# An xDeepFM forward pass on one core: layer 1 of the last five pairs as three fp32r terms

## The chip, the cores and the metric

One core of one Trainium2 chip runs the program. The metric is the device time of one execution in microseconds; the median of three runs is compared. Engines are named as in the profile: PE is the matrix engine, DVE VectorE, ACT ScalarE, POOL GpSimd, SP the engine that issues most DMAs.

## The reference, cut to what matters

512 samples, 26 sparse features with embeddings of 32 values, 13 dense values.

```python
emb = tables[feat_idx, sparse]                      # (512, 26, 32)
linear_out = lin_sparse_w[feat_idx, sparse].sum(-1) + dense @ lin_dense_w
x0 = xk = emb
for w, bb in ((conv1_w, conv1_b), (conv2_w, conv2_b)):   # CIN, 128 outputs each
    hp = einsum('bhd,bmd->bhmd', xk, x0).reshape(-1, h * 26, 32)
    xn = sigmoid(einsum('oi,bid->bod', w, hp) + bb)
    xk = xn[:, :64]; res.append(xn[:, 64:])
cin_out = concatenate(res, 1).sum(-1) @ cin_w + cin_b
h1 = tanh([emb, dense] @ W1 + b1)                   # 845 -> 1024
h2 = tanh(h1 @ W2 + b2)                             # -> 512
h3 = tanh(h2 @ W3 + b3)                             # -> 256
out = linear_out + cin_out + h3 @ deep_w + deep_b + bias
```

## The kernel before, in words

The batch is cut into 16 pairs (NPAIR) of 32 samples. A pair is two chunks c of 16 samples, so 2 x 512 columns of (sample, embedding value).

Gathering: POOL fetches the rows of a pair into emb by seven indirect DMAs (L396); its queue holds the gathers of all 16 pairs first. SP writes them to HBM as laid (L309, L311), and reads them back as raw (L331) and, one feature broadcast over 64 partitions, as copied (L344). For the pairs 0 and 1 SP lays them out directly (L319). ACT (x_high, L640) and DVE (x_low, L766) split raw into a high fp32r part and the rest, both in the tile x.

Layer 1 of the CIN works on squares: a product of two features comes from the square of their sum. PE makes the sums of pairs of features from x with 0/1 weights (sums_of, L455), ACT squares them (squares, L649) into sq, three tiles u of 117 rows for each c, and PE multiplies sq with the weights in fp32 (layer1, L473), two column halves q of 64 outputs each. ACT takes two sigmoids into xk (L660) and one into res1 (L662).

Layer 2 has 13 tiles t per pair. Each needs a product of xk with two features of x, spread over the partitions: in the tiles 2, 3, 6, 7, 8, 11, 12 (COPIED) the features come by DMA into an SBUF buffer copied and DVE multiplies SBUF by SBUF; in the tiles 0, 1, 4, 5, 9, 10 (SPREAD) PE spreads them into PSUM (spread_tile, L485) and DVE multiplies PSUM by SBUF (both L836). PE then multiplies with the weights in fp32 (main, L495), four matmuls a tile in the count of the profile. res2 is taken by ACT (sigmoid2, L670); DVE sums res1 and res2 over the embedding (fold1 L774, fold2 L780), and transposes emb for the deep network (turn, L793, L794).

The order on PE of a pair i is written by hand in three groups: sums(i+1,2), spread tiles 4 and 5, main 0 to 3, layer1(i+1,0); then sums(i+2,0), spread 9 and 10, main 4 to 8, layer1(i+1,1); then sums(i+2,1), spread 0 and 1 of pair i+1, main 9 to 12. Sums and spread tiles share a ring of three PSUM buffers, so spread 9 waits for the product of tile 4 and spread 10 for that of tile 5 (slot_free). DVE starts the products of a pair when the sigmoids of layer1(i,1) are in xk. DVE does x_low(i+2) after tile 5, fold1 after tile 5, turn and fold2(i-1) after tile 9. ACT's order in pair i is sigmoid2(i-1), squares(i+1,2), x_high(i+2), a weight piece, sigmoid(i+1,0), squares(i+2,0), sigmoid(i+1,1), squares(i+2,1).

The deep network runs as three fp32r terms: hi x hi, lo x hi, hi x lo (deep, L516). The weights of its first layer come as 14 pieces of 512 columns, one a pair: SP loads one, ACT writes hi (piece_high, L677), DVE writes lo after tile 11 (piece_low, L787). Its input xt is split in pair 15: hi by ACT (L726), lo by POOL (xt_low, L405), started at the products 0, 4 and 9 of that pair. The first deep tile is worked in between the groups of pair 15; the rest follows, and POOL splits the weights of the later layers beside it (split_piece, L411, L413).

Before the first pair PE multiplies 12 times with unused results (WARM, L545), and twice more after layer1(0,1) (L562).

## Time and profile before

| what | us |
|---|---|
| median of three runs | 420.84 (420.27 to 423.86) |
| the profiled execution, its own time | 420.59 |
| span of its instructions | 418.8 |
| PE busy in the span | 402.7 |
| DVE busy | 311.9 |

The span runs from the first to the last instruction of the profiled execution; 1.8 us lie around it. The clock granted to PE was 0.992 of full over the whole. Steady work begins near 61 us; from there a pair takes 19.42 us, and the last product of pair 15 is multiplied at 350.28 us. The deep network is what is left.

### The profile page before, as it was taken

The numbers are of one execution on the slowest core, as the hardware profiler recorded it, in microseconds if no ns is written. First come the engines' busy times: TensorE is split into PE (matmuls) and PEld (weight loads), VectorE is DVE, ScalarE is ACT, GpSimd is POOL, SyncE is SP. The second block draws the span as 40 slices with busy tenths as digits, with TensorE's granted clock in tenths as the row PEclk, the third lists the DMA queues.
The fourth block names the chain that finished last, engine by engine and source line by source line (L and its number), as shares of the span: only waits on it lengthen the run. The fifth ranks groups of instructions, "written<-read, shape, count | busy, mean of one in ns | idle before, by whom it ended". The sixth has DMA issues, their size and how long they took to land.

```text
span 418.8 us, 5255 instructions
## 1 busy us (share of the span) xinstructions
PE 402.7 (96%) x1854; PEld 167.9 (40%) x1854; DVE 311.9 (74%) x347; ACT 161.9 (39%) x269; POOL 174.6 (42%) x146
## 2 busy tenths in 40 slices
PE   3967999999999999999999999999999999999998
PEld 1412233333333333333333333333333335887885
DVE  4104869998989989898989898998989898432223
ACT  3136445435253544544543525354454511112012
POOL 6745473664844754855656600000000255880000
PEclk9979999999999999999999999999999999999999
DMA  5368689999999999999989998899978670430000
GB/s 203 60 142 177 159 185 227 212 237 235 216 230 224 220 236 237 224 235 212 234 227 219 228 226 233 211 221 214 227 189 200 167 186 2 122 79 2 1 0 2
DMA packets 43582, 73.93 MB, mean 177 GB/s; under 512 B 22206, under 2 KB 24638, under 8 KB 43555
## 3 DMA queue, kind: packets, MB, share of 16 engines
q1 hardware_dynamic: 39970, 71.82, 71.5%
q0 software_dynamic: 3584, 1.76, 3.2%
q8 instruction: 15, 0.25, 0.3%
q14 instruction: 13, 0.10, 0.1%
HBM read 71.63 MB, written 1.71 MB: 175 GB/s over the span
## 4 chain that ended last, share of the span: by engine, by line
PE 88%; issue 4%; ACT 2%; another core or an unknown queue 2%; DMA 1%; SPq 1%; DVE 1%; DVEq 0%; ACTq 0%
PE conv L495 43%; PE conv L473 19%; PE conv L516 8%; PE ring L516 7%; PE ring L485 5%; PE ring L455 4%; ACT xk L660 1%; SPq L319 1%; PE ring L531 1%; ACT x L632 1%; DMA idx_sb<-in_idx 0%; ACT res L662 0%; DMA copied<-emb 0%; DVE prod L836 0%
## 5 line engine op out<-in xcount | busy, mean ns | idle before, releaser
L396 POOL DMA_INDIRECT emb<-in_table,rows x112 | 141.9, 1267 | 96.9 <-DMA emb<-in_table,rows 65.2
L836 DVE TENSOR_TENSOR prod<-ring,xk 128x1024 f32<-128x1024 f32 x96 | 114.2, 1216 | 32.3 <-ACT xk L660 27.4
L836 DVE TENSOR_TENSOR copied<-copied,xk 128x1024 f32<-128x1024 f32 x112 | 135.1, 1243 | 0.0
L495 PE MATMUL conv<-copied,w_sb 128*64 128x512 f32 x448 | 105.2, 593 | 0.0
L660 ACT ACTIVATE xk<-conv,const_sb 64x512 f32<-64x512 f32 x64 | 43.7, 683 | 143.1 <-PE conv L473 117.0
L495 PE MATMUL conv<-prod,w_sb 128*64 128x512 f32 x384 | 93.1, 605 | 2.7 <-DVE prod L836 2.7
L473 PE MATMUL conv<-sq,w_sb 117*64 117x512 f32 x384 | 90.7, 608 | 3.4 <-ACT sq L689 3.4
L495 PEld LDWEIGHTS conv<-copied,w_sb 128*64 128x64 f32 x448 | 31.7, 137 | 63.5 <-issue 55.8
L473 PEld LDWEIGHTS conv<-sq,w_sb 117*64 117x64 f32 x384 | 27.7, 139 | 58.8 <-issue 57.7
L405 POOL TENSOR_TENSOR xt_lo<-xt,xt_hi 128x512 fp32r<-128x512 f32 (+1 forms) x7 | 10.9, 1582 | 96.2 <-ACT xt_hi L726 91.6
L649 ACT ACTIVATE sq<-ring 117x512 f32<-117x512 f32 x90 | 48.6, 595 | 3.9 <-issue 3.2
L495 PEld LDWEIGHTS conv<-prod,w_sb 128*64 128x64 f32 x384 | 23.3, 136 | 47.3 <-issue 42.8
L485 PE MATMUL ring<-x,sel_sb 58*128 58x512 f32 x192 | 32.1, 407 | 0.7 <-ACT sq L649 0.7
L875 DVE CAST h_hi<-hf 128x512 fp32r<-128x512 f32 x8 | 8.2, 1024 | 21.7 <-ACT hf L739 21.7
L455 PEld LDWEIGHTS ring<-x,sel_sb 58*117 58x117 f32 x96 | 8.4, 174 | 36.6 <-issue 35.7
L670 ACT ACTIVATE res<-conv,const_sb 128x512 f32<-128x512 f32 x16 | 11.1, 691 | 31.1 <-PE conv L495 27.9
L455 PE MATMUL ring<-x,sel_sb 58*117 58x512 f32 x96 | 22.9, 481 | 0.0
L662 ACT ACTIVATE res<-conv,const_sb 64x512 f32<-64x512 f32 x32 | 21.9, 684 | 0.8
L485 PEld LDWEIGHTS ring<-x,sel_sb 58*128 58x128 f32 x192 | 17.9, 188 | 10.6 <-issue 4.9
L761 DVE TENSOR_TENSOR x<-copied,x 26x512 fp32r<-26x512 f32 x4 | 2.8, 688 | 23.5 <-issue 15.1
L875 DVE CAST xt_hi<-hf 128x512 fp32r<-128x512 f32 x4 | 1.7, 427 | 17.9 <-ACT hf L739 17.9
L739 ACT ACTIVATE hf<-ring,const_sb 128x512 f32<-128x512 f32 x6 | 4.1, 689 | 26.0 <-PE ring L516 26.0
(99 smaller groups left out, 324.8 us busy)
## 6 DMA issues: line engine op xcount, KB each, us to landing
copied<-laid SPq DMA_DIRECT2D x224, 256.0 KB
wpiece<-in_mlp SPq DMA_DIRECT2D x22, 256.0 KB
raw<-laid SPq DMA_DIRECT2D x56, 52.0 KB
emb<-in_table,rows POOLq DMA_INDIRECT x112, 4.8
laid<-emb SPq DMA_DIRECT2D x16, 96.0 KB
sel_f<-in_sel SPq DMA_DIRECT2D x1, 832.0 KB, 5.6
const_sb<-in_const SPq DMA_DIRECT2D x1, 626.5 KB, 4.1
w_sb<-in_w SPq DMA_DIRECT2D x1, 416.0 KB
```

Source lines behind the costliest of these rows:

```text
L396: pool.indirect_dma_start(out=emb[0:n, i, j, :], out_offset=None, in_=table, in_offset=bass.IndirectOffsetOnAxis(ap=rows[0:n, i, j:j + 1], ...
L405: nc.gpsimd.tensor_tensor(xt_lo[0:n, k, :], xt[0:n, k, :], xt_hi[0:n, k, :].bitcast(F32), ALU.subtract).then_inc(xt_lo_done, 1)
L455: mm = nc.tensor.matmul(sums_bank(i, u)[0:UK, c, :], sel1_sb[at:at + XK, u, :], x[i % RX][at:at + XK, :], start=True, stop=True)
L473: mm = nc.tensor.matmul(l1_bank(i, c)[o, :], w1_sb[:, u, o], sq[i % 2][0:UK, u, c, :], start=(u == 0), stop=(u == UT - 1))
L485: mm = nc.tensor.matmul(spread_bank(r)[:, c, :], sel2_sb[at:at + XK, t, :], x[i % RX][at:at + XK, :], start=True, stop=True)
L495: mm = nc.tensor.matmul(conv[i % 2][c * HALF:(c + 1) * HALF, :], w2_sb[:, t, :], prod_of(r)[:, c, :], start=(t == 0), stop=(t == T2 - 1))
L516: mm = nc.tensor.matmul(MLP_BANKS[n % 2], w[0:r, k, mt * P:(mt + 1) * P], h[0:r, k, :], start=(k == 0 and j == 0), stop=(k == kt - 1 and j ...
L649: nc.scalar.activation(sq[i % 2][0:UK, u, c, :], sums_bank(i, u)[0:UK, c, :], ACT.Square)\
L660: nc.scalar.activation(xk[i % 2][q * HALF:(q + 1) * HALF, c, :], bank[0:HALF, :], ACT.Sigmoid, bias=small_sb[0:HALF, C_CB1:C_CB1 + 1]).the ...
L662: nc.scalar.activation(res1[i % 2][c * HALF:(c + 1) * HALF, :], bank[HALF:P, :], ACT.Sigmoid, bias=small_sb[HALF:P, C_CB1:C_CB1 + 1]).then ...
L670: nc.scalar.activation(res2[i % 2][:, :], conv[i % 2][:, :], ACT.Sigmoid, bias=small_sb[:, C_CB2:C_CB2 + 1]).then_inc(l2_read, 1)
L836: nc.vector.tensor_tensor(prod_of(r)[:, :, :].rearrange("p c n -> p (c n)"), left[:, :, :].rearrange("p c n -> p (c n)"), xk[i % 2][:, :, ...
```

## The change

Layer 1 of the pairs 11 to 15 (SPLIT_FROM) is no longer an fp32 product of 2 x 3 column halves but nine fp32r products over all 128 columns: w_hi x sq_hi and w_lo x sq_hi for each u, then w_hi x sq_lo. For this ACT writes sq_hi after each pair of squares (square_highs, two copies), and sq_lo is written over sq: five of the six tiles of a pair by POOL (LOWS), started when the products 0 (one), 4 (two) and 9 (two) of a pair are reached, and the sixth, (1, 1), by DVE after tile 3 (LOW_AT). The weight split w1_lo is one more instruction at the start.

The space for sq_hi is taken from the low parts of the deep weights. Two of the seven weight tiles (KEEP) are split as before, in four pieces in the pairs 1 to 4. The other five are loaded whole into the place of their high parts in the pairs 4 to 13, and split late, in two sets of five pieces: ACT copies a piece (late_copy), POOL or DVE makes the low part, ACT rounds the high part in place (late_high). The first set lies in pair 14 (two on POOL, three on DVE after tile 12) with its high parts in pair 15; the second lies behind the last product (all on DVE). The last of the seven xt_lo goes from POOL to DVE, after tile 8.

x_low is moved from behind tile 5 to behind tile 3 in the pairs from 1 on. WARM is 9 and the second filler runs once. SP issues the first two copies behind the direct layout of pair 1 instead of ahead of it.

```diff
@@ -50,8 +50,11 @@
 SPREADS_IN = (((0, 4), (0, 5)), ((0, 9), (0, 10)), ((1, 0), (1, 1)))
 SUMS_IN = {0: ((1, 2),), 1: ((2, 0),), 2: ((2, 1),)}
 L1_IN = {0: 0, 1: 1}
-X_LOW_AT, TURN_AT, FOLD1_AT, PIECE_AT = (10, 5), 9, (5, 5), 11
-WARM = 12
+X_LOW_AT, TURN_AT, FOLD1_AT, PIECE_AT = (10, 3), 9, (5, 5), 11
+KEEP = 2
+LOW_AT, LATE_AT, XT_AT = 3, 12, 8
+SPLIT_FROM = 11
+WARM = 9

 C_B1, C_B2, C_B3, C_DEEP, C_CB1, C_CB2, C_CIN1, C_CIN2, C_ONE, C_AUX, C_LOW, C_END = 0, 8, 12, 14, 16, 17, 18, 19, 20, 22, 23, 24
 SMALL_AT = 0
...
@@ -98,17 +102,25 @@
-        m1_hi = sb("m1_hi", [P, K1, D1], F32R)
-        m1_lo = sb("m1_lo", [P, K1, D1], F32R)
+        at_m1 = space(K1 * D1 * 4)
+        m1_hi = sb("m1_hi", [P, K1, D1], F32R, at_m1)
+        m1_f = sb("m1_f", [P, K1, D1], F32, at_m1)
+        m1_kept = sb("m1_kept", [P, KEEP, D1], F32R)
-        at_a = space(2 * K1 * B * 4)
-        sq = [sb(f"sq{k}", [P, UT, 2, CH], F32, at_a + k * UT * 2 * CH * 4) for k in range(2)]
-        xt_hi = sb("xt_hi", [P, K1, B], F32R, at_a)
-        xt_lo = sb("xt_lo", [P, K1, B], F32R, at_a + K1 * B * 4)
+        SQ = UT * 2 * CH * 4
+        LATE = (K1 - KEEP) * D1 * 4
+        at_a = space(4 * SQ)
+        assert LATE + 2 * K1 * B * 4 <= 4 * SQ and LATE <= 2 * SQ
+        sq_hi = [sb(f"sq_hi{k}", [P, UT, 2, CH], F32R, at_a + 2 * k * SQ) for k in range(2)]
+        sq = [sb(f"sq{k}", [P, UT, 2, CH], F32, at_a + (2 * k + 1) * SQ) for k in range(2)]
+        sq_lo = [sb(f"sq_lo{k}", [P, UT, 2, CH], F32R, at_a + (2 * k + 1) * SQ) for k in range(2)]
+        m1_late = sb("m1_late", [P, K1 - KEEP, D1], F32R, at_a)
+        xt_hi = sb("xt_hi", [P, K1, B], F32R, at_a + LATE)
+        xt_lo = sb("xt_lo", [P, K1, B], F32R, at_a + LATE + K1 * B * 4)
...
@@ -183,7 +200,10 @@
-        KW = 2 * K1
+        KW = 2 * KEEP
+        NL = K1 - KEEP
+        LATE_POOL = 2
+        LOWS = ((0, 0), (0, 1), (1, 0), (2, 0), (2, 1))
@@ -223,6 +243,17 @@

             return RAW * (i // RX + (1 if i % RX >= DIRECT else 0))

+        def late(m):
+
+            k, at = KEEP + m % NL, m // NL * WP
+            n = P if k < K1 - 1 else K1_LAST
+            return (m1_f[0:n, k, at:at + WP], mlp1[k * P:k * P + n, at:at + WP],
+                    m1_hi[0:n, k, at:at + WP], m1_late[0:n, k - KEEP, at:at + WP])
+
+        def m1_low(k):
+
+            return m1_kept[:, k, :] if k < KEEP else m1_late[:, k - KEEP, :]
+
@@ -352,11 +395,9 @@
             sp.dma_start(aux[DENSE_AT:DENSE_AT + ND, :], dense_t).then_inc(aux_in, 16)
             direct(0)
             lay_out(0)
-            for n in range(2):
-                copy(n)
             direct(1)
             lay_out(1)
-            for n in range(2, RC):
+            for n in range(RC):
                 copy(n)
             lay_out(2)
             fetch(2)
...

+            def sq_low(i, u, c):
+
+                pool.wait_ge(sq_hi_done, highs_up_to(i, u, c))
+                nc.gpsimd.tensor_tensor(sq_lo[i % 2][0:UK, u, c, :], sq[i % 2][0:UK, u, c, :],
+                                        sq_hi[i % 2][0:UK, u, c, :].bitcast(F32), ALU.subtract)\
+                  .then_inc(sq_lo_done, 1)
+
+            def late_low(m):
+
+                src, _, _, lo = late(m)
+                pool.wait_ge(late_copied, m + 1)
+                nc.gpsimd.tensor_tensor(lo, src, lo.bitcast(F32), ALU.subtract).then_inc(late_lo, 1)
+
...
@@ -418,15 +474,31 @@
+            for i in range(SPLIT_FROM - 2, NPAIR):
+                if SPLIT_FROM <= i + 1:
+                    pool.wait_ge(prod_done, T2 * i)
+                    if i + 1 < NPAIR:
+                        sq_low(i + 1, 1, 0)
+                    else:
+                        xt_low(0)
+                        xt_low(1)
+                    pool.wait_ge(prod_done, T2 * i + 4)
+                    if i + 1 < NPAIR:
+                        sq_low(i + 1, 2, 0)
+                        sq_low(i + 1, 2, 1)
+                    else:
+                        xt_low(2)
+                        xt_low(3)
+                pool.wait_ge(prod_done, T2 * i + 9)
+                if i + 2 < NPAIR:
+                    sq_low(i + 2, 0, 0)
+                    sq_low(i + 2, 0, 1)
+                elif i == NPAIR - 2:
+                    for m in range(LATE_POOL):
+                        late_low(m)
+                else:
+                    xt_low(4)
+                    xt_low(5)
@@ -466,12 +538,29 @@
                     pe.wait_ge(l1_read, 2 * i + 1)
                 if (i, c) == (0, 1):
                     pe.wait_ge(aux_read, 1)
+                bank = l1_bank(i, c)
+                if i < SPLIT_FROM:
+                    for u in range(UT):
+                        pe.wait_ge(sq_done, squares_up_to(i, u, c))
+                        for q in range(2):
+                            o = slice(q * HALF, (q + 1) * HALF)
+                            mm = nc.tensor.matmul(bank[o, :], w1a_sb[:, u, o], sq[i % 2][0:UK, u, c, :],
+                                                  start=(u == 0), stop=(u == UT - 1))
+                    mm.then_inc(l1_done, 1)
+                    return
                 for u in range(UT):
-                    pe.wait_ge(sq_done, squares_up_to(i, u, c))
-                    for q in range(2):
-                        o = slice(q * HALF, (q + 1) * HALF)
-                        mm = nc.tensor.matmul(l1_bank(i, c)[o, :], w1_sb[:, u, o], sq[i % 2][0:UK, u, c, :],
-                                              start=(u == 0), stop=(u == UT - 1))
+                    pe.wait_ge(sq_hi_done, highs_up_to(i, u, c))
+                    nc.tensor.matmul(bank[:, :], w1_hi[:, u, :], sq_hi[i % 2][0:UK, u, c, :],
+                                     start=(u == 0), stop=False)
+                    nc.tensor.matmul(bank[:, :], w1_lo[:, u, :], sq_hi[i % 2][0:UK, u, c, :],
+                                     start=False, stop=False)
+                for u in range(UT):
+                    if (u, c) in LOWS:
+                        pe.wait_ge(sq_lo_done, lows_up_to(i, u, c))
+                    else:
+                        pe.wait_ge(sq_lo_dve, i - SPLIT_FROM + 1)
+                    mm = nc.tensor.matmul(bank[:, :], w1_hi[:, u, :], sq_lo[i % 2][0:UK, u, c, :],
+                                          start=False, stop=(u == UT - 1))
                 mm.then_inc(l1_done, 1)

             def spread_tile(r):
...
@@ -506,14 +595,18 @@
+                if layer == 0:
+                    pe.wait_ge(late_hi, NL * (1 + mt * P // WP))
-                    if n == 0:
+                    if n == 0 and k < K1 - 1:
+                    elif n == 0:
...
@@ -558,7 +651,7 @@
-            for k in range(2):
+            for k in range(1):
@@ -649,6 +742,14 @@
+            def square_highs(i, u):
+
+                if i >= SPLIT_FROM:
+                    for c in range(2):
+                        act.wait_ge(sq_done, squares_up_to(i, u, c))
+                        nc.scalar.activation(sq_hi[i % 2][0:UK, u, c, :], sq[i % 2][0:UK, u, c, :], ACT.Copy)\
+                          .then_inc(sq_hi_done, 1)
+
@@ -669,6 +770,21 @@
+
+            def late_copy(m):
+
+                src, _, _, lo = late(m)
+                act.wait_ge(late_in[m // NL], 16 * NL)
+                nc.scalar.activation(lo, src, ACT.Copy).then_inc(late_copied, 1)
+
+            def late_high(m):
+
+                src, _, hi, _ = late(m)
+                if m < LATE_POOL:
+                    act.wait_ge(late_lo, m + 1)
+                else:
+                    act.wait_ge(late_lo_dve, m - LATE_POOL + 1)
+                nc.scalar.activation(hi, src, ACT.Copy).then_inc(late_hi, 1)
@@ -705,18 +821,25 @@
                 sigmoid2(i - 1)
                 if i + 1 < NPAIR:
                     squares(i + 1, 2)
+                    square_highs(i + 1, 2)
                 if i + 2 < NPAIR:
                     x_high(i + 2)
                 if i <= KW:
                     piece_high(i - 1)
+                if i == NPAIR - 2:
+                    act.wait_ge(l1_done, 2 * (NPAIR - 1))
+                    for m in range(NL):
+                        late_copy(m)
                 if i + 1 < NPAIR:
                     sigmoid(i + 1, 0)
                 if i + 2 < NPAIR:
                     squares(i + 2, 0)
+                    square_highs(i + 2, 0)
                 if i + 1 < NPAIR:
                     sigmoid(i + 1, 1)
                 if i + 2 < NPAIR:
                     squares(i + 2, 1)
+                    square_highs(i + 2, 1)
                 if i == NPAIR - 2:
                     act.wait_ge(l1_done, 2 * NPAIR)
                     act.wait_ge(turned, 2 * NPAIR)
@@ -725,9 +848,15 @@
                         n = P if k < K1 - 1 else K1_LAST
                         nc.scalar.activation(xt_hi[0:n, k, :], xt[0:n, k, :], ACT.Copy).then_inc(xt_hi_done, 1)

+            for m in range(NL):
+                late_high(m)
+            for m in range(NL, 2 * NL):
+                late_copy(m)
             sigmoid2(NPAIR - 1)
             act.wait_ge(lin_done, 1)
             nc.scalar.activation(lin16[:, :], ring[1][0:NPAIR, 1, 0:PB], ACT.Copy).then_inc(lin_copied, 1)
+            for m in range(NL, 2 * NL):
+                late_high(m)

             n = 0
             for layer, bias in enumerate((C_B1, C_B2, C_B3)):
@@ -840,6 +984,16 @@
+                    if t == LOW_AT and SPLIT_FROM <= i + 1 < NPAIR:
+                        sq_low(i + 1, 1, 1)
+                    if t == LATE_AT and i == NPAIR - 2:
+                        for m in range(LATE_POOL, NL):
+                            late_low(m)
+                    if t == XT_AT and i == NPAIR - 1:
+                        dve.wait_ge(xt_hi_done, K1)
+                        nc.vector.tensor_tensor(xt_lo[0:K1_LAST, K1 - 1, :], xt[0:K1_LAST, K1 - 1, :],
+                                                xt_hi[0:K1_LAST, K1 - 1, :].bitcast(F32), ALU.subtract)\
+                          .then_inc(xt_lo_dve, 1)
@@ -854,6 +1008,8 @@
+            for m in range(NL, 2 * NL):
+                late_low(m)
```

In pair i, PE waits in a split layer1 for highs_up_to and, in the last three matmuls, for lows_up_to or sq_lo_dve.

## Rows read from the trace of the kernel before

**Rows 1.** The page, part 1: busy time, share of the span, instructions.
```profile
PE 402.7 (96%) x1854; PEld 167.9 (40%) x1854; DVE 311.9 (74%) x347; ACT 161.9 (39%) x269; POOL 174.6 (42%) x146
```

**Rows 2.** The page, part 4: the chain that ended last, by line.
```profile
PE conv L495 43%; PE conv L473 19%; PE conv L516 8%; PE ring L516 7%; PE ring L485 5%; PE ring L455 4%; ACT xk L660 1%; SPq L319 1%; PE ring L531 1%; ACT x L632 1%; DMA idx_sb<-in_idx 0%; ACT res L662 0%; DMA copied<-emb 0%; DVE prod L836 0%
```

**Rows 3.** The timeline, PE, pair 10: start us, us, engine line op.
```profile
232.69 0.49 PE L455 MATMUL ring<-x,sel_sb 58*117 58x512 f32 x2
...
241.52 2.75 PE L473 MATMUL conv<-sq,w_sb 117*64 117x512 f32 x12
244.20 0.49 PE L455 MATMUL ring<-x,sel_sb 58*117 58x512 f32 x2
...
245.08 1.94 PE L495 MATMUL conv<-prod,w_sb 128*64 128x512 f32 x8
...
252.10 0.49 PE L455 MATMUL ring<-x,sel_sb 58*117 58x512 f32 x2
```

**Rows 4.** The timeline, DVE, pair 10.
```profile
234.23 2.36 DVE L836 TENSOR_TENSOR prod<-ring,xk 128x1024 f32<-128x1024 f32 x2 [1.80 <-ACT xk L660]
236.50 2.35 DVE L836 TENSOR_TENSOR copied<-copied,xk 128x1024 f32<-128x1024 f32 x2
...
241.03 0.74 DVE L766 SCALAR_TENSOR_TENSOR x<-raw,const_sb,x 122x512 fp32r<-122x512 f32 x1
241.70 0.68 DVE L774 TENSOR_REDUCE fold<-res 128x16 f32<-128x512 f32 x1
...
246.83 0.37 DVE L793 STREAM_TRANSPOSE xt<-emb 128x192 f32<-128x192 f32 x1
...
247.21 0.63 DVE L780 TENSOR_REDUCE fold<-res 128x16 f32<-128x512 f32 x1
...
250.04 0.68 DVE L787 TENSOR_TENSOR m_lo<-wpiece,m_hi 128x512 fp32r<-128x512 f32 x1
```

**Rows 5.** The chain in order of time, last part of pair 15: start us, us.
```profile
350.28 2.29 PE conv L516 x9
```

**Rows 6.** The timeline, ACT, pair 10.
```profile
234.93 1.08 ACT L649 ACTIVATE sq<-ring 117x512 f32<-117x512 f32 x2
...
238.81 0.64 ACT L640 ACTIVATE x<-raw 122x512 fp32r<-122x512 f32 x1
```

**Rows 7.** The timeline, ACT, pair 15.
```profile
331.80 3.75 ACT L726 ACTIVATE xt_hi<-xt 128x512 fp32r<-128x512 f32 x7
```

**Rows 8.** The timeline, POOL, pair 15, two looks at single instructions.
```profile
332.58 1.29 POOL L405 TENSOR_TENSOR xt_lo<-xt,xt_hi 128x512 fp32r<-128x512 f32 x1 [91.58 <-ACT xt_hi L726]
...
333.83 2.28 POOL L405 TENSOR_TENSOR xt_lo<-xt,xt_hi 128x512 fp32r<-128x512 f32 x1
```

**Rows 9.** The timeline, DVE, pair 15, looks at single instructions.
```profile
333.37 1.58 DVE L836 TENSOR_TENSOR copied<-copied,xk 128x1024 f32<-128x1024 f32 x1
...
334.88 2.31 DVE L836 TENSOR_TENSOR copied<-copied,xk 128x1024 f32<-128x1024 f32 x1
...
337.11 1.21 DVE L836 TENSOR_TENSOR prod<-ring,xk 128x1024 f32<-128x1024 f32 x1
```

**Rows 10.** Windows, pairs 14 and 15: us, busy time by engine, PEclk, DMA, GB/s.
```profile
310.36:329.56 19.20, 19.20 (x94) 6.42 (x92) 17.31 (x20) 7.36 (x12) 0.00 (x0) 1.00 0.75 188
329.56:352.50 22.94, 22.94 (x104) 8.95 (x102) 20.89 (x19) 7.17 (x12) 10.89 (x7) 1.00 0.53 130
```

**Rows 11.** The timeline, the head, PE and DVE.
```profile
8.50 12.15 PE L545 MATMUL conv<-sel_f 128*128 128x512 f32 x24
...
21.53 0.96 PE L455 MATMUL ring<-x,sel_sb 58*117 58x512 f32 x6
...
35.05 1.98 PE L562 MATMUL ring<-w_sb 128*128 128x512 f32 x4
...
17.69 1.40 DVE L761 TENSOR_TENSOR x<-copied,x 26x512 fp32r<-26x512 f32 x2 [8.36 <-ACT x L632]
```

**Rows 12.** One tile's instructions, h_hi: ns min/median/max.
```profile
L875 DVE CAST h_hi<-hf x8: 426/1358/1465, 353.8 to 387.3; 128x512 fp32r<-128x512 f32 x8
```

62 lines of the change are left out of this document (40 added, 22 removed).

## The prediction

> **What bounds the kernel now.** I read the busy table first: PE is busy 402.7 of 418.8 us, DVE 311.9, ACT 161.9 [rows 1]. The chain that ended last stands on PE for its large parts, 43% main and 19% layer 1 [rows 2], and DVE's products, its last line, hold 0%. The reader is to see in pair 10 how near the second engine is. I take as zero the start of sums(12,1), 232.69; the same point of the next pair is 252.10 [rows 3], so a pair takes 19.42 us, all PE work. In it layer 1 of one c starts at 8.83 and the next work on PE at 11.51: 2.68 us, twice a pair; main 4 starts at 12.39 [rows 3], 0.88 later, the price of sums and two spread tiles. A tile of main is what is left, (19.42 - 2 x 2.68 - 3 x 0.88) / 13 = 0.88. DVE has 13 products at 1.135 (two in 2.27), x_low 0.67, fold1 0.60, turn 0.38, fold2 0.56 and piece_low 0.60 [rows 4]: 14.76 + 2.81 = 17.57 us. It waits 1.80 us for xk, and starts tile 0 at 1.54 [rows 4]. So DVE has 1.8 us to spare in 19.4. What is new in the pairs 10 to 14 is that POOL, silent there once its gathers are done, computes beside DVE; only pair 15 shows what that costs.
>
> **The split layer 1.** Nine fp32r matmuls after main took 2.29 us, 350.28 on, those of the deep network with nearly the same shape [rows 5]. Against 2.68 that saves 0.39, ten times (two for each of the pairs 11 to 15, worked in PE's pairs 10 to 14): 3.9 us, if PE never waits. PE's own work in a pair becomes 19.42 - 0.78 = 18.64 us.
>
> **ACT.** Six more copies a pair; seven took 3.75 us, 0.54 each [rows 7], so 3.2 us on an engine with over 9 us free. The squares (i+1,1) are issued at 2.24 and take 1.08 [rows 6]; the first copy behind them is done at 3.9. x_high starts at 6.12 and takes 0.64 [rows 6]; two copies now stand ahead of it: done at 6.12 + 1.08 + 0.64 = 7.84. The copies of (i+2,0) and (i+2,1) fall in the gaps before the next sigmoids.
>
> **POOL beside DVE.** In pair 15 a low part on POOL takes 1.29 us, beside a product from PSUM (1.21, its usual) [rows 8, 9]. The next one began at 333.83 and took 2.28; DVE's two SBUF products around it took 1.58 and 2.31 instead of 1.21 [rows 8, 9]. Laid end to end this is one at a time: POOL to 333.88, product, POOL, product. So an operation of DVE with two SBUF inputs and one of POOL go in turn, each whole. x_low and the DVE sq_low also have two SBUF inputs; that they queue too no row shows. Bounds for what the two lows after tile 3 cost DVE there: 0, and 2.66 as worked below. I take 2.66, since the nearest rows are SBUF by SBUF. The Trainium skill, SBUF — State Buffer, section "Who interferes with whom", says that a DVE instruction with two SBUF inputs and a GpSimd one that reads SBUF exclude each other for the whole instruction, the first to start having the port. By this rule the sum is my forecast; with a port that only the wide products feel it is the fast rival below.
>
> **A pair from 10 to 13, step by step** (from the pair's zero). POOL's low part of the square tile u = 1, c = 0 of the next pair, written (i+1,1,0), is free to start at product 0 but waits for the copy at 3.9: it works 3.93 to 5.22. In pair 10 DVE is on time, tile 2 has the port at 3.81, POOL goes 4.94 to 6.23, tile 3 ends at 7.36. In the later pairs DVE is late, tile 2 waits until 5.22 and tile 3 ends at 7.49. Now DVE wants x_low, which needs x_high: 7.84. POOL wants (i+1,2,0), released by the same tile 3, at 7.57, and has the port until 8.86. x_low to 9.53, POOL's second low to 10.82, sq_low to 11.42. Without POOL that is 7.49 + 1.27 = 8.76: cost 2.66. Tile 4 ends at 12.56, tile 5 at 13.69. PE's spread 10 waits for tile 5, where PE would be there at 11.7 (8.83 + 2.29 + about 0.6); one spread tile later, at 14.05, main 4 starts; five tiles 4.39, 0.1 for tile 8, layer 1 2.29: the next zero at 20.83, xk at 22.37. DVE after tile 5 has 0.60 + 3.40 + 1.13 + 0.94 + 3.40 = 9.48 and ends at 23.17, 0.80 late. That fits its own sum: 17.57 (sq_low in place of piece_low) + 0.61 before tile 2 + 2.66 = 20.84. The two lows after tile 8 fall beside tiles 9 and 10, from PSUM: nothing. So pair 10 takes 20.7, pairs 11 to 13 20.84: 83.2 against 77.7, **+5.5 us**. The saved PE time is gone and DVE sets the pace.
>
> **Pair 14** has no x_low, so the DVE sq_low has the port first, 7.49 to 8.09, and POOL's lows lie beside tiles 4 and 5. PE: 19.20 [rows 10] - 0.78, **-0.8 us**.
>
> **Pair 15.** In pair 14 DVE goes on from 8.09 with 9.48 + 2.27 + 0.38 for the second turn and ends at 20.2, 1.8 us after the next zero at 18.42. Three late lows of 0.60 follow before tile 0; xk was ready at 1.54. If POOL's first xt_low, free at 2.95, comes behind the third, tile 1 ends at 5.9 instead of 3.9; if before it, at 7.2. Spread 5 wants it near 4.4 (0.9 and four tiles). Bounds 0 and +2.8; I take **+1.3** on the 22.94 [rows 10], as the race is even and 1.5 is its good end, less what small waits of today it swallows. late_high on ACT ends near 9.4 (xt_hi at 2.24 + 3.75, then sigmoid2 and five copies), PE wants it at 8.6 + 1.3: covered. The second late set: DVE's five (3 us) after the products delay ACT's five copies and so the first tanh by some 3 us, but deep tile 1 (21 matmuls, near 5 us) is worked meanwhile: 0; uncovered it would be 3.
>
> **The head.** 12 fillers run 8.50 to 20.65, and the sums start at 21.53; they need x_low, done at 17.69 + 1.40 = 19.09 [rows 11]. Three fillers less are 3.0 us at their mean of 1.01, of which 2.4 counts. The other filler: 2 took 1.98 [rows 11], behind layer1(0,1); one less saves 0 to 0.99, I take 0.9. **-3.3 us**, bounds 0 (if something else holds the first squares back) and -4.0 (all four in full). The split of w1 is one 0.5 us operation on an idle DVE. The first two copies are needed some 20 us after their old issue: 0; the direct layout of pair 1 and its gathers get free earlier. x_low behind tile 3 in the pairs 1 to 9 waits 0.7 for x_high, out of DVE's 1.8: 0, and 0.7 a pair if that were used up.
>
> **Sum**: 420.6 - 3.3 + 5.5 - 0.8 + 1.3 = **423.3 us** for the profiled execution. Its 420.59 is within 0.3 of the median, 420.84, so I give the same. My bound of what can be told from no change is 1%: 416.6 and 425.0.
>
> **The rivals.** *x_low wins the race* after tile 3: only 0.27 us decide. For it: ACT and POOL latencies of 0.1 are my guess. Against: pair 10 has 0.4 in POOL's favour. Then x_low ends at 8.16, POOL 9.45, sq_low 10.05, tile 5 12.32: 1.37 less in four pairs, 5.5: **417.8**. *The port hardly matters for x_low and sq_low*: PE stays the bound, four pairs at 18.64 are -3.1, pair 14 -0.8, pair 15 +0.5, head -3.3: **413.9**. For it: no row shows these operations blocked. Against: the products were, exactly in turn. *Slower*: the two lows after tile 8 also block turn and fold2, one-input operations. For it: the DVE cast of h_hi, one input, took 1358 ns beside POOL, 426 alone [rows 12]. They would stand between the two lows and wait 0.2 + 1.3 = 1.5 us in each of the pairs 10 to 13, where DVE has nothing left: +6.0, **429.3**. It decides as soon as turn starts while POOL works, at 18.8 against 19.0. Against: alone, the cast takes 0.43 us for 512 columns and the reduction 0.63 [rows 4, 12], so they are not the same kind of work. The same section of the Trainium skill says that only the two-port modes of DVE, and two SBUF inputs, exclude GpSimd, and a reduction never does; by it this rival costs nothing. *The change doesn't act*: PE's fp32r layer 1 as slow as fp32 would take 3.9 from the fast cases and nothing from mine, where DVE is the bound.
>
> **How the numbers follow.** Forecast 0.42, its own range 421 to 426.5; x_low first 0.16; free port 0.24; slower 0.10; near 420 from mixtures 0.08. The range goes from 413 to 428, which leaves out the slow rival and less than a tenth below. Faster by over 1%: the free port and some of x_low first, 0.28. Slower: 0.10 and 0.13 from the upper part of the forecast, 0.23. Within: 0.49.
>
> **What would show it.** Zeros of the pairs 10 to 14 some 20.8 us apart, DVE with no idle in them; x_low and sq_low of DVE at about 1.3 to 1.9 us in place of 0.7; PE waiting before L485 for DVE in each; layer 1 at 2.3 us; pairs 2 to 9 unchanged at 19.42; steady work 3.3 us earlier. Wrong: pairs near 18.6, or fold2 stretched to 1.9.

## The result and the profile after

Beside each other on one chip, the changed kernel took 431.77 us (431.14 to 432.56) and the kernel before 421.55 us: ratio 1.023, 95% interval 1.019 to 1.027. It is slower, by some 10 us. I had said 423.3, within 1% of before. A second comparison on another chip gave the same ratio (after_2, 1.023, 1.018 to 1.029). Ratios, here and below, leave out executions over 1.5% above the fastest of the same kernel, among them single ones of 685 to 1045 us, of the kernel before too.

The page of the changed kernel, part 1 (against [rows 1]), and the start of part 4, the chain by engine:

```profile
PE 404.2 (94%) x1816; PEld 174.3 (41%) x1816; DVE 327.1 (76%) x352; ACT 183.9 (43%) x309; POOL 203.2 (47%) x172
PE 79%; DVE 6%; ACT 4%; issue 3%; another core or an unknown queue 3%; POOL 2%; DMA 1%; DVEq 0%; ACTq 0%; POOLq 0%
```

PE's busy time is no lower, though its layer 1 got shorter and four fillers are gone: it stood at half clock for 20.5 us in three stretches, against 6.8 us before. DVE has 15 us more.

The profiled execution took 432.04 us against 420.59, 11.45 more. I laid it out by four marks in both timelines: the start of tile 0 of pair 2 on DVE, the zeros of pair 10 and of pair 14 on PE (the start of the sums from which the prediction counts), and the linear term's first matmul behind pair 15.

| stretch | before | after | difference | predicted |
|---|---|---|---|---|
| start to tile 0 of pair 2 | 78.86 | 83.04 | +4.2 | -3.3 |
| from there to the zero of pair 10 | 153.83 | 153.87 | 0.0 | 0 |
| pairs 10 to 13 | 77.67 | 84.81 | +7.1 | +5.5 |
| pairs 14 and 15, to the linear term | 42.14 | 42.23 | +0.1 | +0.5 |
| deep layers, to the end | 66.28 | 66.28 | 0.0 | 0 |

So the split's pairs came out as forecast in kind and 1.6 us dearer, and the head came out 7.5 us over its forecast: it lost 4.2 us instead of gaining 3.3.

First the pairs. PE, timeline of pair 12 of the changed kernel, the lines that answer to [rows 3]:

```profile
280.47 0.49 PE L527 MATMUL ring<-x,sel_sb 58*117 58x512 f32 x2
...
289.41 0.50 PE L553 MATMUL conv<-sq_hi,w_hi 117*128 117x512 f32 x1
...
290.90 0.86 PE L562 MATMUL conv<-sq_lo,w_hi 117*128 117x512 f32 x3
291.69 0.49 PE L527 MATMUL ring<-x,sel_sb 58*117 58x512 f32 x2
292.50 0.49 PE L574 MATMUL ring<-x,sel_sb 58*128 58x512 f32 x2 [0.32 <-DVE prod L980]
293.63 0.50 PE L574 MATMUL ring<-x,sel_sb 58*128 58x512 f32 x2 [0.64 <-DVE prod L980]
...
300.91 0.49 PE L527 MATMUL ring<-x,sel_sb 58*117 58x512 f32 x2
```

Layer 1 of one c runs from 289.41 to 291.69, 2.28 us: the 2.29 that I had taken from the deep layers [rows 5]. Behind it stand two waits for DVE's products. The pair takes 20.44 us.

DVE (answering to [rows 4]) and POOL in the same pair, two timelines:

```profile
284.27 3.44 DVE L980 TENSOR_TENSOR copied<-copied,xk 128x1024 f32<-128x1024 f32 x2
288.30 1.31 DVE L895 SCALAR_TENSOR_TENSOR x<-raw,const_sb,x 122x512 fp32r<-122x512 f32 x1 [0.59 <-ACT x L733]
289.54 1.77 DVE L921 TENSOR_TENSOR sq_lo<-sq,sq_hi 117x512 fp32r<-117x512 f32 x1
...
297.50 1.21 DVE L980 TENSOR_TENSOR prod<-ring,xk 128x1024 f32<-128x1024 f32 x1
298.63 0.36 DVE L934 STREAM_TRANSPOSE xt<-emb 128x192 f32<-128x192 f32 x1
...
299.02 0.63 DVE L909 TENSOR_REDUCE fold<-res 128x16 f32<-128x512 f32 x1
```

```profile
284.58 2.05 POOL L447 TENSOR_TENSOR sq_lo<-sq,sq_hi 117x512 fp32r<-117x512 f32 x1 [6.43 <-ACT sq_hi L750]
287.79 2.98 POOL L447 TENSOR_TENSOR sq_lo<-sq,sq_hi 117x512 fp32r<-117x512 f32 x2 [1.16 <-ACT sq_hi L750]
297.65 2.53 POOL L447 TENSOR_TENSOR sq_lo<-sq,sq_hi 117x512 fp32r<-117x512 f32 x2 [6.89 <-DVE copied L980]
```

The reader is to see three things. Two SBUF products take 3.44 us instead of 2.35, where POOL's first low part begins. x_low takes 1.31 and DVE's sq_low 1.77, where they would be 0.74 and 0.68, while POOL works 287.79 to 290.77. And beside POOL's last two, 297.65 to 300.18, the transpose (0.36) and the reduction (0.63) are as short as in [rows 4].

Now pair 10, POOL's timeline, and what DVE did beside it:

```profile
228.44 1.42 POOL L439 DMA_INDIRECT emb<-in_table,rows  x1 [5.14 <-DMA emb<-in_table,rows]
...
239.14 0.90 POOL L439 DMA_INDIRECT emb<-in_table,rows  x1 [0.30 <-issue]
240.14 3.77 POOL L447 TENSOR_TENSOR sq_lo<-sq,sq_hi 117x512 fp32r<-117x512 f32 x3
```

```profile
240.72 5.41 DVE L980 TENSOR_TENSOR copied<-copied,xk 128x1024 f32<-128x1024 f32 x2
240.72 4.28 DVE L980 TENSOR_TENSOR copied<-copied,xk 128x1024 f32<-128x1024 f32 x1
246.06 0.74 DVE L895 SCALAR_TENSOR_TENSOR x<-raw,const_sb,x 122x512 fp32r<-122x512 f32 x1
```

The last set of gathers ends at 240.04 and three low parts that were free to start run in one go. DVE's first SBUF product waits for all three (the second line is that product alone): 5.41 - 2.35 = 3.06 us lost. With tile 3 that late, x_high is there, and x_low starts ahead of POOL's next low part (246.06 against 246.21) and takes 0.74: the one pair with low parts in this trace in which x_low comes first. From the start of tile 0 of pair 10 to that of pair 11 it is 21.69, not 20.7. (From here on "pair n" gives this distance from tile 0 to tile 0 on DVE; in it PE works layer 1 of pair n + 1. Pair 11 takes 21.85: a stretch of 3.4 us at half clock from 272.3 on is in it, behind waits of PE for DVE of 0.68 and 0.64 us; pair 13 has nearly the same waits and no such stretch. Pairs 12 and 13 take 20.98 and 20.81.)

The head: the timelines of PE and ACT in the changed kernel.

```profile
19.54 0.96 PE L527 MATMUL ring<-x,sel_sb 58*117 58x512 f32 x6
24.00 1.98 PE L547 MATMUL conv<-sq,const_sb 117*64 117x512 f32 x4 [3.51 <-issue]
26.32 3.68 PE L547 MATMUL conv<-sq,const_sb 117*64 117x512 f32 x8 [0.34 <-ACT sq L805]
29.93 0.74 PE L574 MATMUL ring<-x,sel_sb 58*128 58x512 f32 x4
...
40.22 0.78 PE L527 MATMUL ring<-x,sel_sb 58*117 58x512 f32 x2 [5.77 <-DVE x L890]
```

```profile
23.26 0.60 ACT L805 ACTIVATE sq<-ring 117x512 f32<-117x512 f32 x1 [4.95 <-remote]
25.67 0.60 ACT L805 ACTIVATE sq<-ring 117x512 f32<-117x512 f32 x1 [1.81 <-remote]
27.09 2.06 ACT L805 ACTIVATE sq<-ring 117x512 f32<-117x512 f32 x4 [0.82 <-remote]
...
35.91 1.39 ACT L761 ACTIVATE xk<-conv,const_sb 64x512 f32<-64x512 f32 x2 [6.33 <-remote]
37.32 0.68 ACT L763 ACTIVATE res<-conv,const_sb 64x512 f32<-64x512 f32 x1
38.03 1.28 ACT L725 ACTIVATE x<-copied 26x512 fp32r<-26x512 f32 x2
```

And ACT in the kernel before:

```profile
25.16 3.04 ACT L689 ACTIVATE sq<-ring 117x512 f32<-117x512 f32 x6 [6.85 <-remote]
...
31.39 1.39 ACT L660 ACTIVATE xk<-conv,const_sb 64x512 f32<-64x512 f32 x2 [2.77 <-PE conv L473]
```

The sums do start 2.0 us earlier than in [rows 11]. But before, all six squares followed one another from 25.16; here they come singly, and the first xk comes 4.5 us later though PE's records of layer 1 for it end at 30.0. x_high of pair 1 stands behind xk on ACT, x_low behind x_high, PE's sums behind x_low: PE idles 5.77 us. The same window of the head, after and then before (the third number from the end is the granted clock, 0.67 against 0.83):

```profile
25.00:45.00 20.00, 12.76 (x40) 3.25 (x38) 5.61 (x6) 9.67 (x17) 9.85 (x11) 0.67 0.81 176
```

```profile
25.00:45.00 20.00, 16.36 (x56) 4.89 (x56) 6.39 (x7) 12.06 (x21) 11.21 (x12) 0.83 0.66 139
```

### The profile page after: what moved, and what is told of

It is laid out like the page before. It is cut to its first block, busy times and chain, and to the rows that moved or that the text cites. A ratio compares the mean times of both kernels' runs of the same rounds, so it can differ in the third digit from the quotient of the medians.

```text
span 430.2 us, 5277 instructions
## 1 busy us (share of the span) xinstructions
PE 404.2 (94%) x1816; PEld 174.3 (41%) x1816; DVE 327.1 (76%) x352; ACT 183.9 (43%) x309; POOL 203.2 (47%) x172
## 4 chain that ended last, share of the span: by engine, by line
PE 79%; DVE 6%; ACT 4%; issue 3%; another core or an unknown queue 3%; POOL 2%; DMA 1%; DVEq 0%; ACTq 0%; POOLq 0%
PE conv L584 39%; PE conv L547 12%; PE conv L609 8%; PE ring L609 7%; PE ring L574 5%; PE ring L527 4%; DVE prod L980 3%; POOL emb L439 2%; DVE sq_lo L921 1%; PE conv L553 1%; DVE copied L980 1%; ACT xk L761 1%; PE conv L562 1%; PE conv L555 1%
## 5 line engine op out<-in xcount | busy, mean ns | idle before, releaser
L439 POOL DMA_INDIRECT emb<-in_table,rows x112 | 134.9, 1205 | 102.9 <-DMA emb<-in_table,rows 69.2
L980 DVE TENSOR_TENSOR copied<-copied,xk 128x1024 f32<-128x1024 f32 x112 | 138.6, 1281 | 0.0
L584 PE MATMUL conv<-prod,w_sb 128*64 128x512 f32 x384 | 96.5, 623 | 1.1 <-DVE prod L980 1.1
L547 PE MATMUL conv<-sq,const_sb 117*64 117x512 f32 x264 | 63.5, 616 | 3.9 <-issue 3.5
L447 POOL TENSOR_TENSOR sq_lo<-sq,sq_hi 117x512 fp32r<-117x512 f32 x25 | 35.0, 1421 | 57.3 <-DVE copied L980 35.1
L584 PEld LDWEIGHTS conv<-copied,w_sb 128*64 128x64 f32 x448 | 31.4, 138 | 66.7 <-issue 49.7
L574 PE MATMUL ring<-x,sel_sb 58*128 58x512 f32 x192 | 33.3, 411 | 4.9 <-DVE prod L980 4.2
L547 PEld LDWEIGHTS conv<-sq,const_sb 117*64 117x64 f32 x264 | 18.8, 140 | 42.5 <-issue 40.4
L771 ACT ACTIVATE res<-conv,const_sb 128x512 f32<-128x512 f32 x16 | 11.0, 689 | 20.8 <-PE conv L584 17.8
L1031 DVE CAST h_hi<-hf 128x512 fp32r<-128x512 f32 x8 | 4.1, 507 | 19.4 <-ACT hf L868 19.4
L895 DVE SCALAR_TENSOR_TENSOR x<-raw,const_sb,x 122x512 fp32r<-122x512 f32 x14 | 12.9, 922 | 6.1 <-ACT x L733 6.1
L750 ACT ACTIVATE sq_hi<-sq 117x512 fp32r<-117x512 f32 x30 | 17.3, 628 | 0.2
```

What stands on the lines that cost most here:

```text
L439: pool.indirect_dma_start(out=emb[0:n, i, j, :], out_offset=None, in_=table, in_offset=bass.IndirectOffsetOnAxis(ap=rows[0:n, i, j:j + 1], ...
L447: nc.gpsimd.tensor_tensor(sq_lo[i % 2][0:UK, u, c, :], sq[i % 2][0:UK, u, c, :], sq_hi[i % 2][0:UK, u, c, :].bitcast(F32), ALU.subtract)\
L547: mm = nc.tensor.matmul(bank[o, :], w1a_sb[:, u, o], sq[i % 2][0:UK, u, c, :], start=(u == 0), stop=(u == UT - 1))
L574: mm = nc.tensor.matmul(spread_bank(r)[:, c, :], sel2_sb[at:at + XK, t, :], x[i % RX][at:at + XK, :], start=True, stop=True)
L584: mm = nc.tensor.matmul(conv[i % 2][c * HALF:(c + 1) * HALF, :], w2_sb[:, t, :], prod_of(r)[:, c, :], start=(t == 0), stop=(t == T2 - 1))
L750: nc.scalar.activation(sq_hi[i % 2][0:UK, u, c, :], sq[i % 2][0:UK, u, c, :], ACT.Copy)\
```

## The experiments

The chips differ in the head: on some, tile 0 of pair 0 starts at 38.8 us or later (the pair of traces above, after_2, and the runs with it), on others at 28.5 to 31.5, in the kernel before too (before_newhead is that kernel but for three edits of the head). I call them late and early chips; on early ones before takes some 417 to 418.6 us. Between 18 and 30 us the granted clock is 1.00 in every early trace and 0.72 to 0.88 in every late one. Neither the kernel before nor the changed kernel as it is was traced on an early chip. Ratios are against before on the same chip.

**1. The head's edits undone in the changed kernel**, on an early chip.

```
-WARM = 9
+WARM = 12                                        (h_warm, h_all)
-            for k in range(1):
+            for k in range(2):                   (h_filler, h_all)
+            for n in range(2):                   (h_copies, h_all)
+                copy(n)
             direct(1)
             lay_out(1)
-            for n in range(RC):
+            for n in range(2, RC):
```

h_all: 

> The changed kernel with the whole head of the one before: 12 fillers, two later fillers, first two copies at their old place. In the changed kernel tile 0 of pair 1 starts at 64.26 us against 60.07 before. Theory A (three fillers less leave PE slow: its sums then came at 23.3, 25.7 and 27.1 us, and its first layer 1 ended at 35.9 against 31.3): tile 0 of pair 1 back at 60.1, time 4.2 less than the changed kernel, about 427.5. Rival B (the move of the copies delays pair 1): the same here, told apart by the next two. Rival C (the split of w1 and the new wait ahead of layer 1 do it): no gain, 431.8.

h_warm: 

> The changed kernel with 12 fillers alone (WARM). Theory A: most of the 4.2 us comes back, tile 0 of pair 1 near 60 to 61, the three first sums done within 0.1 us of each other near 25.1; time 427.5 to 428.5. Rival B (copies): no gain or worse, 431.8 or up to 2.5 more, as the fillers only add their time.

h_copies: 

> The changed kernel with the first two copies at their old place alone. Theory A: no gain, 431.8. Rival B: back by up to 4.2, 427.6.

h_filler: 

> The changed kernel with the later filler twice again (9 fillers ahead, old value 12). Theory A says PE's clock in pair 0 is what counts: PE waits 5.8 us for x_low(1) behind this filler and then works at half clock from 36.8 to 47.0; one more filler of about 1 us shortens that wait and may keep the clock: 0 to 2 us less, 430 to 431.8. Rival B: 431.8.

| kernel | ratio to before | tile 0 of pair 2 | pair 10 | last gather, after tile 0 of pair 10 |
|---|---|---|---|---|
| h_copies | 1.020 (1.017 to 1.023) | 78.3 | 20.76 | +1.9 |
| h_all | 1.042 (1.038 to 1.047) | 78.9 | 27.96 | +5.8 |
| h_filler | 1.048 (1.044 to 1.052) | 77.3 | 31.27 | +12.8 |
| h_warm | 1.053 (1.050 to 1.055) | 78.6 | 34.67 | +16.3 |

These say nothing of the head, since on this chip pair 2 starts at 77 to 79 whatever is done, and the first xk comes at 23.8 with early copies and 23.4 with late ones (h_copies, h_filler). They showed something I had left out: pair 10 grows up to 35 us, with the start of the last gather. h_warm's PE waits 9.6 us there for POOL's sq_lo; in h_all it is DVE that waits, 7.30 us for an x_low of 0.75 beside five low parts in a row. The time also moves within one kernel: of the four executions of h_copies two took 425.2 and 426.3 and two, not in its ratio, 437.0 and 446.7; one of h_filler took 455.0. That fits gathers that end at another time in each execution, but only one execution of each was traced.

**2. The same kernels again, and the split from pair 12.** A late chip.

```
-SPLIT_FROM = 11
+SPLIT_FROM = 12                                  (s12, s12_x5)
-X_LOW_AT, TURN_AT, FOLD1_AT, PIECE_AT = (10, 3), 9, (5, 5), 11
+X_LOW_AT, TURN_AT, FOLD1_AT, PIECE_AT = (10, 5), 9, (5, 5), 11      (s12_x5)
```

before_2: 

> The kernel before, for its trace on the chip of this call. If pair 1 starts near 60 and pair 2 near 79 again, the head is bound there as in the first trace (PE); if tile 0 of pair 0 starts near 31 instead of 38.8, as in the four runs of the changed head, PE is faster in the head of this chip and pair 2 is bound by x(3), which comes by DMA: start near 78 in every variant.

after_2: 

> The changed kernel again. Theory D (the last gathers stand ahead of the first low parts in POOL's queue): the end of the gathers, 240 us in its first trace, moves from run to run with the DMAs, between 236.6 and 251 in the four variants; pair 10 lasts as long as it has to wait, 20.8 if they end by 237, 21.7 at 240, 28 or more beyond, and the time of the kernel moves with it by up to 14 us. Rival: pair 10 is lengthened by the port alone, then it is 20.8 in every run.

s12: 

> SPLIT_FROM = 12: pair 11 keeps its fp32 layer 1, so the first low parts are wanted 19.4 us later, when the gathers are through. Theory D: pair 10 at 19.42, pairs 11 to 13 at 20.8 each by the port, pair 14 and 15 as before; time below the changed kernel by 1.3 to 14 us, by what pair 10 lost, and the rounds lie within 1 us. Rival (port alone): 1.4 less and no narrower.

s12_x5: 

> The same with x_low behind tile 5 again. By the port's turns (forecast): sq_low of DVE goes ahead of POOL's two lows, which fall beside tiles 4 and 5 from PSUM; x_low waits some 0.3 only: pairs 11 to 13 at 18.7 to 19.1 instead of 20.8, 5 to 6 us less than s12. Rival (the cost of the pairs is DVE's load or PE, not the order after tile 3): no change, 20.8.

before_2 took 422.1, the pairs 10 to 13 19.42 each. after_2: the gathers were done before pair 10 (last start 224.8), and pair 10 took 20.97, like 11 to 13 (20.8). From the zero of pair 10 to that of pair 14 it is 82.85 us, 5.2 over before, where I had said 5.5. But its head is worse than in the first trace: the first xk at 38.0 and tile 0 of pair 2 at 88.2, 7.7 us behind before_2; s12 and s12_x5, on the same chip, are 2.4 and 2.9 behind. s12, 1.019 (1.014 to 1.025): pair 10 is 19.41 again, then 20.98, 20.80, 20.79. **s12_x5, 1.002 (1.000 to 1.005)**: pairs 11 to 13 take 18.79, 18.79, 18.84. Moving one 0.7 us operation behind two more products gives back 2.0 us a pair, 6.5 us between the medians (429.8 and 423.3). The timelines of DVE and POOL in pair 12 of s12_x5:

```profile
279.21 3.44 DVE L980 TENSOR_TENSOR copied<-copied,xk 128x1024 f32<-128x1024 f32 x2
282.57 0.68 DVE L921 TENSOR_TENSOR sq_lo<-sq,sq_hi 117x512 fp32r<-117x512 f32 x1
283.17 2.34 DVE L980 TENSOR_TENSOR prod<-ring,xk 128x1024 f32<-128x1024 f32 x2
285.44 0.75 DVE L895 SCALAR_TENSOR_TENSOR x<-raw,const_sb,x 122x512 fp32r<-122x512 f32 x1
```

```profile
282.72 2.91 POOL L447 TENSOR_TENSOR sq_lo<-sq,sq_hi 117x512 fp32r<-117x512 f32 x2 [1.16 <-ACT sq_hi L750]
```

Here DVE doesn't wait for x_high, so its sq_low starts before POOL's two low parts (282.57 against 282.72) and takes 0.68. POOL's pair lies beside products that read PSUM, 2.34 for two; x_low comes when it is over, 0.75. The wait for the first low part (3.44) is still there and costs nothing: PE sets the pace.

**3. Low parts that read nothing**, and the head on s12_x5. A late chip.

```
-                nc.gpsimd.tensor_tensor(sq_lo[...], sq[...], sq_hi[...].bitcast(F32), ALU.subtract)
+                nc.gpsimd.memset(sq_lo[...].bitcast(F32), 0.0)      (s12_memset)
```

s12_memset: 

> s12 (x_low behind tile 3), where GpSimd's five low parts of the squares are replaced by memsets of the same tiles: GpSimd writes, but reads nothing from SBUF. It leaves out those low parts, so their terms add zero. Theory that a GpSimd operation that reads SBUF and a DVE operation with two SBUF inputs go in turn: x_low back at 0.67 to 0.75 us, sq_low at 0.6 to 0.7, no PE wait for DVE behind tile 5, the pairs 12 to 14 at 18.7 to 18.9, the time near that of s12_x5 (423). Rival, x_low and sq_low at tile 3 are slow for another reason (their place beside x_high and copies, DVE's own load): pairs stay at 20.8 and the time at 429 to 430. Between: memsets write through the same port and still block, at their own length.

Measured 1.002 (0.998 to 1.005), pairs 12 and 13 at 18.80 with x_low still behind tile 3 (pair 11 at 19.31, which I had at 18.7 to 18.9). DVE's and POOL's timelines:

```profile
279.98 2.34 DVE L978 TENSOR_TENSOR copied<-copied,xk 128x1024 f32<-128x1024 f32 x2
283.50 0.75 DVE L893 SCALAR_TENSOR_TENSOR x<-raw,const_sb,x 122x512 fp32r<-122x512 f32 x1 [1.18 <-ACT x L731]
284.17 0.68 DVE L919 TENSOR_TENSOR sq_lo<-sq,sq_hi 117x512 fp32r<-117x512 f32 x1
```

```profile
279.75 0.53 POOL L447 MEMSET sq_lo<- 117x512 f32 x1 [6.38 <-ACT sq_hi L748]
282.55 0.99 POOL L447 MEMSET sq_lo<- 117x512 f32 x2 [2.27 <-ACT sq_hi L748]
```

x_low waits longer for x_high than in the changed kernel (1.18 against 0.59) and the pair is still at 18.8: what costs the 2 us is POOL's low parts, not where x_low stands by itself. The SBUF products keep 2.34, though the first of them starts within the first memset, at 279.98. The other two memsets are over at 283.54, before they could meet x_low, so this run doesn't separate "reads nothing" from "is short".

x5_oldhead is s12_x5 with all three edits of the head undone, x5_warm with 12 fillers alone, x5_copies with the old copy order alone. Their expectations name pairs by their layer 1, one more than the table's counting.

x5_oldhead: 

> s12_x5 with the whole old head (12 fillers, two later ones, the first two copies ahead of the direct layout). Theory: what is left of the change's loss beside the pairs 12 to 14 sits in the head and in the tail; with the old head, tile 0 of pair 0 comes at 38.8 instead of 40.7 and tile 0 of pair 2 at 79 to 80.5 instead of 83.3, and the time is 2 to 4 us under s12_x5, 419 to 421, 0 to 2 us under before (ratio 0.995 to 1.000). Rival: the head is only moved by chance from run to run (before_2 began its pair 2 at 80.4, before at 78.9), then this and s12_x5 give the same time within 1 us. The pairs 10 and 11 at 19.4, 12 to 14 at 18.8 by both.

x5_warm: 

> s12_x5 with 12 fillers again, copies and the later filler as in the changed kernel. Theory that the three fillers carry the head: tile 0 of pair 0 at 38.8, and most of the gain of x5_oldhead (2 us or more under s12_x5). Rival, the order of the first copies carries it: no gain (within 1 us of s12_x5), and x5_copies has it all.

x5_copies: 

> s12_x5 with the first two copies issued at their old place, 9 fillers. Theory that the fillers carry the head: within 1 us of s12_x5, tile 0 of pair 0 at 40.7. Rival, the copies carry it: 2 us or more less, through pair 1, which took 23.5 to 23.9 in the changed head and 21.3 to 22.8 in the old one.

| kernel, late chips | ratio | first xk | tile 0 of pair 0 | tile 0 of pair 2 | half clock |
|---|---|---|---|---|---|
| s12_x5 (new head) | 1.002 (1.000 to 1.005) | 35.82 | 40.7 | 83.3 | 10.2 and 6.8 us |
| x5_warm | 1.005 (1.001 to 1.009) | 36.20 | 41.8 | 81.8 | 13.7 us |
| x5_copies | 0.993 (0.988 to 0.998) | 31.04 | 39.0 | 81.5 | 6.8 and 3.4 us |
| x5_oldhead | 0.997 (0.994 to 1.001) | 32.56 | 39.3 | 79.3 | 6.8 us |

s12_x5 ran on another chip than the other three; s12_memset, on theirs and with the same new head, reached pair 2 at 83.6. The head's edits cost 4.0 us in the profiled executions (83.3 against 79.3), but less in the medians (423.5 for s12_memset, 421.7 for x5_oldhead, 1.8 us), and the ratios' intervals overlap. Neither edit alone has it all: I had put it on the fillers, and x5_warm got 1.5 us in its trace and nothing in its ratio; the rival, all on the copies, got 1.8. The later filler was not put back alone on a late chip. The split of w1 is still in x5_oldhead, and x_low stands behind tile 3 in s12 and behind tile 5 in s12_x5 (82.8 and 83.3), so neither of these carries the loss.

x5_copies' interval is below x5_oldhead's median, but its twelve times scatter from 416.4 to 428.0, the four highest (422.9 to 428.0) are not in the ratio, and the medians of all twelve are 422.1 and 421.7, so I don't rank the two.

What goes with the copy order in every trace of a late chip is the first xk: 35.8 to 38.0 in all six with late copies (after, after_2, s12, s12_x5, s12_memset, x5_warm), 31.0 to 32.6 in all four with early ones (before, before_2, x5_copies, x5_oldhead). With late copies ACT's first two squares also come singly, with early ones all six in a row. On early chips they come in a row by either order. PE's waits ahead of its first products differ with the fillers. PE's timelines of x5_copies, and of x5_oldhead, which has three more fillers and the second later one,

```profile
40.37 1.97 PE L586 MATMUL conv<-prod,w_sb 128*64 128x512 f32 x4 [4.53 <-DVE prod L982]
```

```profile
40.63 1.08 PE L586 MATMUL conv<-prod,w_sb 128*64 128x512 f32 x4 [2.25 <-DVE prod L982]
```

show four matmuls in 1.97 us, at half clock, behind a wait of 4.53, and in 1.08 behind one of 2.25. So the fillers were not plain work in the way: with them the idle stretch ahead of the products is shorter. It is no sharp rule: before_2, with all of them, had a second stretch of 3.4 us too, and reached pair 2 at 80.4.

**4. The new head alone, and the last gathers moved.** All on early chips.

before_newhead: 

> The kernel before with the three edits of the head alone (9 fillers, one later filler, the first two copies behind the direct layout of pair 1). If the head costs by itself what the accounting says: tile 0 of pair 2 near 83, a stretch at half clock from about 37 to 41 us on, and the time 3 to 4.5 us over before (ratio 1.007 to 1.011). If the head is only slow together with the rest of the change (split of w1, x_low earlier): tile 0 of pair 2 at 79 to 80.5 and the time within 1 us of before. What I predicted blind, -3.3, would be 417.

before_newhead_2: 

> The same kernel as before_newhead. Where tile 0 of pair 0 comes at 38 or later (the late start of the first traces), the theory that the new head costs by itself gives tile 0 of pair 2 near 83 and a ratio of 1.007 to 1.011; the rival, that it costs only beside the rest of the change, gives 79 to 80.5 and 0.998 to 1.002. Where tile 0 of pair 0 comes near 29, it tells nothing new: 1.000 as in before_newhead.

Measured 1.000 (0.997 to 1.003) and 1.000 (0.997 to 1.002). Tile 0 of pair 0 came at 28.6 and 28.5, the second 2.9 us ahead of x5_oldhead_2's 31.4 (the 12-filler head on the same chip): this is the 3.3 us that I had forecast, nearly. By pair 2 it is 76.2 against 77.6, of which the times show nothing. ACT's waits for DMA in the second one, 28 to 80 us, point to why:

```profile
ACT x L638 <- DMA raw<-laid: 13.0, 2, 6.9
```

x5_oldhead_2 waits 11.8 us there for the same transfers, so on an early chip the head's end is set by transfers in either head. Whether the new head costs 4 us in the kernel before on a late chip was not seen.

```
-            for i in range(NPAIR):
+            for i in range(NPAIR - 1):
                 gather(i)
...
                         sq_low(i + 1, 2, 1)
+                    if i == SPLIT_FROM - 1:
+                        gather(NPAIR - 1)
```

h_warm_gather (h_warm with this edit) and h_warm_again:

> h_warm with the last set of gathers behind the first five low parts. Theory: the last gather starts before 238 ahead of the low parts, no PE wait of several us for sq_lo, pair 10 at 20.7 to 21.3, no stretch at half clock there. If PE's wait in pair 10 has another cause: 27 to 35 us as in h_warm.

> The same kernel as h_warm, as control beside h_warm_gather. Theory: pair 10's length follows the start of the last gather less the start of tile 0 of pair 10 (+2 gave 20.8, +0.7 gave 21.7, +5.8 gave 28.0, +12.8 gave 31.3, +16.2 gave 34.7, -18.8 gave 21.0): under +1 it is 20.8 to 21.7, over +5 it is 27 or more. Rival: pair 10 is long whenever 12 fillers stand in the head, whatever the gathers do.

One execution each. h_warm_again: 437.5 us, pair 10 at 33.69, last gather 15.1 us after its tile 0, PE waiting 8.35 us. h_warm_gather: 425.7 us, pair 10 at 23.52, no wait for sq_lo. PE's timeline of the one and of the other at the same point of the work:

```profile
250.27 0.79 PE L562 MATMUL conv<-sq_lo,w_hi 117*128 117x512 f32 x1 [8.35 <-POOL sq_lo L447]
```

```profile
242.52 0.86 PE L564 MATMUL conv<-sq_lo,w_hi 117*128 117x512 f32 x3
```

The theory holds, and my size for it fails: 23.52, not 20.7 to 21.3. The gathers, now issued until 252.5, stand ahead of two low parts of the next pair, and these meet the last SBUF products of pair 10, 4.90 us in place of 2.34:

```profile
252.33 4.90 DVE L982 TENSOR_TENSOR copied<-copied,xk 128x1024 f32<-128x1024 f32 x2
```

s11_x5_gather shows where that goes when one more low part is held back.

s11_x5_gather (the changed kernel with the old head, x_low behind tile 5, and this edit): 

> The changed kernel with the old head, x_low behind tile 5 and the last set of gathers issued behind GpSimd's first five low parts. By the theory that port turns and the gathers in the way are all that the pairs 10 to 13 lost: pairs 10, 11, 12, 13 at 18.8 each, so 1.2 us less than x5_oldhead and 2 us under before: ratio 0.992 to 0.997, some 420. If gathers (landing, their queue) don't matter, pair 10 is the same as without the move, at 19 to 22. If the late gathers make copies or the turn of pair 15 late, a wait in the pairs 12 to 14 shows it.

Measured 1.000 (0.997 to 1.003); pairs 10 to 13 take 18.79, 20.93, 18.67, 18.79. POOL and DVE in pair 11:

```profile
252.66 3.76 POOL L449 TENSOR_TENSOR sq_lo<-sq,sq_hi 117x512 fp32r<-117x512 f32 x3
```

```profile
252.94 4.58 DVE L984 TENSOR_TENSOR copied<-copied,xk 128x1024 f32<-128x1024 f32 x1
```

The first of DVE's two products takes 4.58 us alone.

Pair 10 gains as expected. Then three low parts held back by the gathers meet two SBUF products, as in pair 10 of the changed kernel, and pair 11 loses 2.1 us: 77.2 us for the pairs 10 to 13, against 75.8 in x5_oldhead.

**5. The best version again.**

x5_oldhead_2: 

> The same kernel as x5_oldhead: pairs 12 to 14 at 18.8, the head as before. By the sum of its parts (three pairs 0.63 shorter, nothing lost elsewhere) 1.5 to 1.9 us under before, ratio 0.9955 to 0.9965; rival: the gain is given back somewhere (copies or DMAs late), ratio 0.999 or more.

417.3 us against 418.6, ratio 0.9975 (0.9956 to 0.9994). Split from pair 12 on, x_low where it was, the head as it was: this version is faster than both kernels, by a quarter of a per cent over before; the interval only just leaves out no change, and that of x5_oldhead (0.994 to 1.001) doesn't. Its pairs 11 to 13 are at 18.79, 18.79, 18.83 (-1.9 us together), the next one at 20.13 against 19.2. That one gives half of the gain back, and by it I missed the 1.5 to 1.9 us that I had expected.

## Why the prediction was wrong

**The head: failed.** "Three fillers less are 3.0 us at their mean, of which 2.4 counts", and "the first two copies are needed some 20 us after their old issue: 0". My bounds for the head were 0 and -4.0; it cost 4.2 us in the first pair of traces, 2.4 to 7.7 in the three of the next chip. Both halves failed on late chips: late copies go with a first xk 3 to 7 us later, which I hadn't allowed any price, and fewer fillers with more idle time on PE ahead of its first products and a second stretch at half clock (6.8 us in s12_x5, 3.4 in x5_copies, none in x5_oldhead). I had read the fillers as work in PE's way and had not asked what the clock would do without them. On early chips the fillers' gain was there (2.9 us at tile 0) and was swallowed by DMA waits. Why late copies delay the squares and the first xk stays open: the changed kernel's chain of waits gives the stretch to nothing that the profile shows,

```profile
18.31 4.93 another core or an unknown queue
29.58 6.25 another core or an unknown queue
```

and PE's records end long before ACT is let go (30.0 and 35.9; in x5_warm, at half clock throughout, they end at 36.1 and xk starts at 36.2, so there the lag is PE's own). The head's loss was seen beside the rest of the change and in s12_x5, never by itself.

**The pairs 10 to 13: right in mechanism, 1.6 us short.** 20.84 was forecast for the pairs 11 to 13, and 20.98 and 20.81 measured in the two that nothing else disturbed; PE waits ahead of its spread tiles; in pair 12 DVE has no idle time but 0.59 for x_high and 0.97 for xk. (The sums that start at my zero are sums(11,1), not sums(12,1); nothing hangs on the name.) Step by step in pair 12, from PE's zero: tile 3 ends at 7.24 (7.49 forecast), POOL has the port from 7.32, x_low ends at 9.14 (9.53), sq_low at 10.84 (11.42), tile 5 at 13.11 (13.69). The two low parts after tile 3 cost 2.33 us (2.66 forecast) and the first one 1.09 (0.61); the errors nearly cancel, and that the sum fits so closely is in part luck. The step that failed is in "POOL, silent there once its gathers are done": in pair 10 they are not done. The low parts stand behind the last set of gathers, which ended 1.6 us into pair 10's products; three lows in one go cost 3.06 us where I had one at 0.61. This makes pair 10 21.7 (20.7 forecast), and up to 34.7 where the gathers come later; in after_2, where they were done, the pairs 10 to 13 cost 5.2 us. Pair 11's 21.85 has a stretch at half clock in it, about 1 us over its neighbours, that no row of before pointed to. These two, about 1 us each, cover the 1.6 us.

**The port: held.** That x_low and sq_low wait for POOL was argued from products alone. The runs bear it out: 1.31 and 1.77 us beside POOL, 0.75 and 0.68 away from it, and so in s12 and s12_x5, which differ in their order alone (1.32 and 1.78, 0.76 and 0.68, in pair 11). The Trainium skill, SBUF — State Buffer, section "Who interferes with whom", says that a DVE operation with two SBUF inputs and a GpSimd operation that reads SBUF exclude each other for their whole length; the traces agree (two products take 3.44 us beside one low part, 5.41 beside three, 2.35 alone).

**The rivals.** x_low lost the race at tile 3 in the pairs 11 to 13, where x_high was late by 0.22, 0.59 and 0.22 us; it won it in pair 10 alone, behind a tile 3 that the three low parts had held back. A free port is refuted by s12 against s12_x5. The slower rival, blocked turn and fold2, had a chance of 0.10 and is refuted: 0.36 and 0.63 us beside POOL. The kernel was slower for reasons that none of my rivals held. That the split doesn't act is refuted too: 2.28 us, and pairs of 18.79 where PE sets the pace, 0.63 below 19.42 (0.78 forecast).

**Pairs 14 and 15, the late set: near.** +0.1 against +0.5; the shares of the two pairs, -0.8 and +1.3, were not told apart. The three late lows run ahead of tile 0 of pair 15 as forecast (1.88 us in all) and what follows is covered. The second late set costs nothing: 66.28 us from the linear term to the end in both.

**The range.** 428 was too low an upper end: my slower cases were all on the port, and none held a head that gets dearer or gathers that still run.

## What to carry to other kernels

Before moving work to a second engine, list what stands ahead of it in that engine's program order, gathers that wait for DMAs above all, and ask how far their end moves from run to run. Where two engines take turns at a port, the order decides and not the load: one small operation that needn't wait, put first, was worth 2 us a pair. Before removing a filler, ask what idle time of the same engine takes its place and at which clock the next work then starts; here the answer differed between chips.

## What was not expected of the hardware

A gather's issue occupies POOL 0.9 to 3.2 us with 0.3 between in the changed kernel's trace, and with the wait for the rows before a set of seven takes 11 to 18 us; the end of the last set lay at 240.0 in one trace of the changed kernel and at 225.7 in the other. Three POOL operations in a row kept one SBUF product of DVE waiting for all of them (4.28 us in the changed kernel's pair 10, 4.58 in s11_x5_gather), and five kept x_low (7.30 in h_all), where in pair 12 x_low got in between POOL's two; what decides whether DVE gets its turn, no run tells. And chips differ by 7.8 us in when the first product starts in the same kernel (31.4 against 39.3, x5_oldhead), though before's medians lie within 6 us (417.3 to 423.2).
